# Who multiplies an edge's one-hot by its digits: VectorE as before, or GpSimd

## The reference, cut to what matters

```python
h = _L0_tok_ref(x, ...)                                   # (64, 64, 64): 4096 nodes
h = h + _L0_attn_ref(_layernorm(h), ...)                  # window attention, 8 heads of 8
h = h + _L0_ffn_ref(_layernorm(h), ..., L0_ffn_edge_index)

# inside _L0_ffn_ref: a graph attention over the edges decides each node's experts
src = concatenate([edge_index[0], loops]); dst = concatenate([edge_index[1], loops])
e = leaky_relu(a_src[src] + a_dst[dst], 0.2)
ee = exp(e - segment_max(e, dst)[dst])
alpha = ee / (segment_sum(ee, dst)[dst] + 1e-16)
agg = segment_sum(h[src] * alpha[:, :, None], dst) + b_gat
```

## Time and profile before

| what | value |
|---|---|
| median of the runs | 905.33 us |
| profiled execution, its own time | 901.5 us |
| its span, first to last instruction | 899.7 us |
| busy in the span: TensorE, VectorE, ScalarE, GpSimd | 64%, 65%, 30%, 37% |
| window attention, first key product to last subtraction | 72.0 to 307.2 us |
| of it, chunks made by VectorE | 186.3 to 268.8 us |

### The profile page before, as it was taken

One profiled execution on the slowest core, in us unless ns is written; L12 is line 12 of the kernel. 1 busy time (PEld: TensorE's weight loads), 2 busy tenths in 40 slices (PEclk: granted clock), 3 DMA queues, 4 the chain that ended last, 5 costly groups with the idle time before them and its releaser, 6 DMA issues. The chain is left out here.

```text
span 899.7 us, 12066 instructions
## 1 busy us (share of the span) xinstructions
PE 573.7 (64%) x4179; PEld 341.4 (38%) x4179; DVE 582.3 (65%) x1272; ACT 267.7 (30%) x485; POOL 337.4 (37%) x387
## 2 busy tenths in 40 slices
PE   5427779666789764154665346561875774588886
PEld 4314446344566454022222122210874552422332
DVE  7976999999995675587556264637443336555663
ACT  1133223122224331033323031321015343365553
POOL 5023123122334222667774677750003210224344
PEclk9996555556689755565555655555556995579998
DMA  6100000000000003212121111100000000000001
GB/s 175 27 1 1 1 1 1 1 0 2 1 1 1 3 1 50 39 21 37 23 37 32 9 32 29 23 7 0 1 0 1 1 1 1 0 1 0 13 13 24
DMA packets 29161, 13.74 MB, mean 15 GB/s; under 512 B 22353, under 2 KB 26290, under 8 KB 28851
## 3 DMA queue, kind: packets, MB, share of 16 engines
q1 hardware_dynamic: 23858, 11.35, 5.0%
q0 software_dynamic: 5248, 1.68, 2.6%
HBM read 11.46 MB, written 1.55 MB: 14 GB/s over the span
## 5 line engine op out<-in xcount | busy, mean ns | idle before, releaser
L1423 POOL DMA_INDIRECT edge_src_row<-src_rows_dram,slot_src_index x160 | 173.5, 1084 | 57.4 <-issue 48.0
L600 POOL TENSOR_TENSOR wa_scores<-wa_scores,wa_max 128x512 f32<-128x512 f32 x32 | 37.1, 1160 | 160.9 <-DVE wa_max L781 160.9
L491 POOL TENSOR_TENSOR ln_xs<-xn,ln_stats 128x256 f32<-128x256 f32 x32 | 21.2, 672 | 153.5 <-DVE ln_stats L459 94.3
L645 PE MATMUL wa_s_ps<-wa_kbd,wa_qk 64*64 64x512 f32 x128 | 54.9, 945 | 27.4 <-issue 27.4
L544 PE MATMUL ln_pT<-ident,ln_xs 128*64 128x128 f32 (+1 forms) x112 | 27.7, 410 | 49.2 <-POOL ln_xs L491 48.5
L1537 PE MATMUL moe_h_ps<-xT,moe_w 65*128 65x512 f32 x64 | 57.0, 1041 | 0.0
L2016 POOL TENSOR_TENSOR moe_acc<-moe_acc,moe_weighted 128x512 f32<-128x512 f32 x28 | 37.8, 1349 | 47.4 <-DVE moe_weighted L1957 47.3
L1265 DVE TENSOR_TENSOR edge_e<-edge_src_row,edge_dst_row 128x40 f32<-128x40 f32 x16 | 3.2, 200 | 76.3 <-DMA edge_src_row<-src_rows_dram,slot_src_index 76.2
L1957 DVE SCALAR_TENSOR_TENSOR moe_weighted<-moe_y_ps,moe_b_cols,moe_G 128x512 f32<-128x512 f32 x32 | 24.0, 751 | 42.9 <-ACT moe_G L1930 40.7
L738 ACT ACTIVATE wa_probsT<-wa_t_ps 128x512 f32<-128x512 f32 x32 | 19.1, 597 | 105.9 <-PE wa_t_ps L653 105.9
L113 DVE TENSOR_TENSOR edge_scratch<-edge_scratch,last_dst_lo 128x3072 bf16<-128x3072 bf16 x28 | 49.0, 1751 | 0.0
(11 more groups left out here) (377 smaller groups left out, 1425.1 us busy)
## 6 DMA issues: line engine op xcount, KB each, us to landing
edge_onehot_T<-slot_lo_dram SPq DMA_DIRECT2D x16, 320.0 KB, 3.5
edge_src_row<-src_rows_dram,slot_src_index POOLq DMA_INDIRECT x160, 2.5
edge_scratch<-in_L_ffn_edge_index SPq DMA_DIRECT2D x2, 1024.0 KB, 6.1
xrow<-in_x SPq DMA_DIRECT2D x4, 256.0 KB, 7.9
out_h<-h SPq DMA_DIRECT2D x4, 256.0 KB, 2.6
moe_w<-in_L_ffn_W SPq DMA_DIRECT2D x3, 256.0 KB
src_rows_dram<-src_rows SPq DMA_DIRECT2D x1, 320.0 KB
moe_w<-in_L_ffn_W SPq DMA_DIRECT2D x2, 128.0 KB
```

The lines of the kernel that those rows point to most:

```text
L600: pool.tensor_tensor(sc[b][:], sc[b][:], bc(mx[b][:], WIN), ALU.subtract).then_inc(shifted, 1)
L645: ins = pe.matmul(s_ps[b][half], qk[b][half, 0, :], kbd[b][half])
L1423: pool.indirect_dma_start(gs[b][:, j, :], None, srow_dram, bass.IndirectOffsetOnAxis(edges.src_index[:, x:x + 1], axis=0))\
```

## The change

The two multiplications of a chunk go from VectorE to GpSimd. GpSimd's loop over pairs of tiles is written out, tile by tile, since the work now differs from tile to tile, and a new function `weigh(pool, c)` is called after `shift(c)`; it does something for c = 15 to 24 only, two chunks in each. The unweighted columns get a second buffer, as two engines now share them. A new semaphore `at_ready` tells GpSimd that a chunk's columns are compared, another, `weighed`, counts GpSimd's multiplications; VectorE waits for it before it writes a buffer of columns again, and TensorE before its matmuls. The generator's condition on `now` is restated.

```diff
--- before.py
+++ after.py
@@ -603,13 +603,10 @@
                 keys(b, b, True)
             for b in range(2):
                 shift(b, b)
-            with pool.Fori(0, n // 2 - 2) as i:
-                for b in range(2):
-                    keys(2 * i + b + 2, b, False)
-                    shift(2 * i + b + 2, b)
-            for b in range(2):
-                keys(n - 2 + b, b, False)
-                shift(n - 2 + b, b)
+            for c in range(2, n):
+                keys(c, c % 2, False)
+                shift(c, c % 2)
+                edges.weigh(pool, c)
 
         @block.tensor
         def _(pe):
@@ -851,10 +848,10 @@
         self.lim = mem.sb("edge_limits", [P, 2], I32)
         self.limits = mem.sb("edge_trips", [P, 2], I32)
         (self.loaded, self.step, self.reduced, self.counted, self.found_more, self.passed, self.filled,
-         self.bucketed, self.prefixed, self.move_ready, self.moved, self.decoded, self.turned, self.turned_out,
+         self.bucketed, self.prefixed, self.at_ready, self.weighed, self.move_ready, self.moved, self.decoded, self.turned, self.turned_out,
          self.lo_stored, self.onehot_ready) = (mem.sem("edges_" + x) for x in (
              "loaded", "step", "rest_reduced", "rest_counted", "more_found", "vector_waits_passed", "reach_filled",
-             "bucketed", "prefixed", "move_ready", "moved", "decoded", "lo_turned", "lo_turned_out", "lo_stored",
+             "bucketed", "prefixed", "at_ready", "weighed", "move_ready", "moved", "decoded", "lo_turned", "lo_turned_out", "lo_stored",
              "onehot_ready"))
         self.done = 0
         self.now = -1
@@ -880,8 +877,9 @@
         self.to_col = [room[:, b * col:(b + 1) * col].bitcast(F16)\
                        .rearrange("p (y c q x) -> p y c q x", y=2, c=GCH // 2, x=2) for b in range(RING)]
         room = room[:, RING * col:]
-        self.at_col = room[:, 0:col // 2].bitcast(F16).rearrange("p (c q x) -> p c q x", c=GCH // 2, x=2)
-        room = room[:, col // 2:]
+        self.at_col = [room[:, b * col // 2:(b + 1) * col // 2].bitcast(F16)\
+                       .rearrange("p (c q x) -> p c q x", c=GCH // 2, x=2) for b in range(2)]
+        room = room[:, col:]
         self.move16 = [room[:, x * RC:(x + 1) * RC].bitcast(F16) for x in range(4)]
 
     def constants(self, pool):
@@ -1030,18 +1028,16 @@
         for j in range(FOUND_CHUNKS):
             assert self.now < MOVE_STEP + j // MOVES, (j, self.now)
             wide = PER * (reach(j)[1] - reach(j)[0])
-            while self.now <= MOVE_STEP + (j - RING) // MOVES:
+            while self.now <= MOVE_STEP + (j - RING) // MOVES or self.now < MOVE_STEP - 2 + j // MOVES:
                 take_last()
                 yield
             if j >= RING:
                 dve.wait_ge(self.moved, j - RING + 1)
             part, iota = slice(GCH * j, GCH * j + GCH), self.iota_rep[:]
-            row, col, at = self.to_row[j % RING], self.to_col[j % RING], self.at_col[:, :, 0:wide]
-            equal(dve, row, iota, row16[:, part]).then_inc(self.move_ready, 1)
-            self.after(dve, equal(dve, at, iota, col16[:, part]))
-            weighted_by(dve, col[:, 0, :, 0:wide], at, high16[:, part]).then_inc(self.move_ready, 1)
-            self.after(dve, weighted_by(dve, col[:, 1, :, 0:wide], at, low16[:, part]))
-            dve.sem_inc(self.move_ready, 1)
+            equal(dve, self.to_row[j % RING], iota, row16[:, part]).then_inc(self.move_ready, 1)
+            if j > 1:
+                dve.wait_ge(self.weighed, 2 * j - 2)
+            equal(dve, self.at_col[j % 2][:, :, 0:wide], iota, col16[:, part]).then_inc(self.at_ready, 1)
             yield
 
         while self.now < TURN_STEP:
@@ -1097,6 +1093,19 @@
         self.after(dve, dve.tensor_copy(self.last_lo[:], digit))
         yield
 
+    def weigh(self, pool, c):
+
+
+        if MOVE_STEP <= c < MOVE_STEP + FOUND_CHUNKS // MOVES:
+            for j in range(MOVES * (c - MOVE_STEP), MOVES * (c - MOVE_STEP + 1)):
+                part, wide = slice(GCH * j, GCH * j + GCH), PER * (reach(j)[1] - reach(j)[0])
+                pool.wait_ge(self.at_ready, j + 1)
+                if j >= RING:
+                    pool.wait_ge(self.moved, j - RING + 1)
+                col, at = self.to_col[j % RING], self.at_col[j % 2][:, :, 0:wide]
+                weighted_by(pool, col[:, 0, :, 0:wide], at, self.move16[2][:, part]).then_inc(self.weighed, 1)
+                weighted_by(pool, col[:, 1, :, 0:wide], at, self.move16[3][:, part]).then_inc(self.weighed, 1)
+
     def multiply(self, pe, c, k):
 
 
@@ -1111,7 +1120,8 @@
         if MOVE_STEP <= c < MOVE_STEP + FOUND_CHUNKS // MOVES:
             for j in range(MOVES * (c - MOVE_STEP), MOVES * (c - MOVE_STEP + 1)):
                 low, high = reach(j)
-                pe.wait_ge(self.move_ready, 3 * (j + 1))
+                pe.wait_ge(self.move_ready, j + 1)
+                pe.wait_ge(self.weighed, 2 * j + 2)
                 for i in range(GCH):
                     ins = pe.matmul(slots[:, :, PER * low:PER * high], self.to_row[j % RING][:, i // 2, :, i % 2],
                                     self.to_col[j % RING][:, :, i // 2, 0:PER * (high - low), i % 2], start=False,
```

## The result

| | before | after |
|---|---|---|
| median of 4 runs each | 905.87 us (904.64 to 911.16) | 943.44 us (937.93 to 947.49) |
| ratio of the times | 1 | 1.0399, 95% interval 1.0326 to 1.0472 |
| profiled execution, span | 901.5, 899.7 us | 937.9, 936.1 us |

What follows compares the result with a forecast made beforehand. The prediction took VectorE to bound attention where it has list work, elsewhere a ring of dependent steps. Longer intervals (+34) and clock recovery (+0.5) on 905.3 gave 940 us; range 918 to 955, the forecast's own 931 to 949.

Steps and rivals of the forecast that it cites:

- The weighing: The forty multiplications moved to GpSimd, four per tile for tiles 15 to 24, predicted to delay the next tile's keys.
- the ring: Window attention's dependent steps: GpSimd's subtraction and keys, TensorE's scores, VectorE's bias and maximum; 4.75 us per turn at clock 1.00.
- Its price: GpSimd's time for the forty multiplications, at 1.69 ns an element plus 0.178 us each: 47.1 us back to back.
- Both rivals on the price: GpSimd's multiplication at half price, 0.84 ns an element (919 us, chance 0.10), or dearer, 2.3 ns (955 us, 0.10).
- The turns: GpSimd's operations and VectorE's comparisons exclude each other at SBUF: 1.1 us per weighing interval, 7.7 us over intervals 17 to 24.
- The clock: TensorE's granted clock in the attention stage, said to decide between totals of +28.1 and +35.2 us.
- the slow end: The total taken for a low granted TensorE clock in the long attention intervals: +34 us.
- Interval 19: From GpSimd's subtraction of tile 19 to the next; predicted at some 12.5 to 13.3 us instead of 8.4.
- the ring of 5.64: One turn of the dependent attention steps with 0.70 of TensorE's clock granted, against 4.75 us at 1.00.
- Intervals 14 to 16: Attention stretches between GpSimd's subtractions: 14 loses four multiplications, -1.1 us; 15 and 16 gain +2.8 us behind VectorE's wait.
- The unrolling is free: Writing out GpSimd's attention loop was taken as 0 us, with up to 2 kept for the range.
- Hidden in GpSimd's idle time: Rival: the multiplications fit into GpSimd's 68.5 us of waiting for VectorE's maximum, giving 884 us; chance 0.05.

Runs made afterwards that it cites:

- twice: The changed kernel, but GpSimd does each of its 40 multiplications twice, writing the same values again; ratio 1.0907 to the kernel before.
- half: The changed kernel, but GpSimd multiplies by the high digit only and VectorE by the low one; ratio 1.0105 to the kernel before.
- order_buffers: The changed kernel with four buffers of unweighted columns and GpSimd's multiplications moved after keys(c+1), before shift(c+1); ratio 1.0013 to the kernel before.
- takes_first: The kernel before, with VectorE's MAX8 and MATCH_REPLACE8 moved ahead of the comparisons in tiles 13 to 15; ratio 0.9979 to the kernel before.
- buffers: The changed kernel with four buffers of unweighted columns instead of two, GpSimd's order unchanged; ratio 1.0386 to the kernel before.
- unroll: The kernel before with GpSimd's window attention loop written out tile by tile, VectorE still multiplying; ratio 0.9997 to the kernel before.

## Why the prediction was right

- **The weighing is in the ring.** Shown by twice and half (0.93 and 0.83 us for one), and from the other side by order_buffers, which takes it out of the ring and gets nearly all of it back.
- **Its price.** 47.1 us were predicted; undisturbed multiplications took 1.58 us for 840 elements and 1.65 for 880 (1.60 and 1.67 by the line through the float32 rows), and 0.58 for 240. With the turns counted in, the group has 50.5. Both rivals on the price, 0.84 and 2.3 ns an element, fall: it is 1.66 to 1.69. One premise of this went unsaid. In all the float32 rows with two inputs, one input is repeated along the tile, as a digit is in `weighted_by`. Where both inputs are full tensors, 512 elements take GpSimd more than 1.04 us, in the same trace of before:

```profile
L2016 POOL TENSOR_TENSOR moe_acc<-moe_acc,moe_weighted x28: 1260/1270/1652, 805.8 to 892.4; 128x512 f32<-128x512 f32 x28
```

By that row, 2.1 ns an element with the same fixed part, the weighing would have come out some 11 us dearer (an estimate). The rows chosen were the ones alike, but the prediction gives no reason for choosing them; whether the repeated input makes the difference was not tested.
- **The turns.** 0.37 and 0.45 us at the fourth multiplication and the keys, where I had 0.35 and 0.43. takes_first shows that they come from VectorE's comparisons. The way to the 0.43 was wrong, and its size partly luck: the 1.42 us show 0.14 us hidden, not 0.26, as 0.52 us of the comparison were left when the subtraction started and it grew by 0.38. The keys met not 0.69 us of a comparison but 0.59: the comparison had itself waited and ended at 249.90, the fourth multiplication at 249.34.
- **The clock.** I took the slow end. Interval 19 came to 13.16 (I had said 12.5 to 13.3), 17 to 24 to 92.9 (86.1 to 93.2), with 0.67 granted. The scores of interval 19 took 1.97 us instead of 1.08, and these 0.89 us are all that parts the ring of 5.64 from that of 4.75. After them interval 25 took 5.64 instead of 4.75, 0.9 where I had put 0.5; but not for the reason given. The clock was at 0.95 and the scores took 1.08 us. It is the keys that started late, as the queries that they need came late from TensorE through ScalarE:

```profile
311.67 1.04 POOL L594 TENSOR_TENSOR wa_kbd<-wa_qk,headmask 128x512 f32<-128x512 f32 x1 [0.84 <-ACT wa_qk L712]
```

- **Intervals 14 to 16.** 7.75, 10.42 and 12.15; I had 8.15, 10.7 and 12.5. That VectorE's wait costs at 15 and 16, as the sum has it, is what buffers shows.
- **The unrolling is free.** Shown.
- **The forecast's distance.** The total was +34.5 against +37.6 by medians and +36.4 by profiles. The stage accounts for 33.9 in intervals 14 to 24 and 0.9 in the rest; the 1.6 us left lie outside these intervals and were not looked into.
- **Hidden in GpSimd's idle time** (the rival on the faster side) is wrong for this program. Its mechanism is real with another order and more buffers, but its price was not: even then GpSimd's own work is as long as what VectorE was relieved from, and the turns come on top (order_buffers, interval 19).

## What to carry to other kernels

Idle time of an engine that waits for the answer to its own work is not room. Before moving work into it, follow its program order and ask whether what others wait for is queued behind the new work. Two edits that each remove one of two waits in parallel may have to be made together to show anything. Where VectorE and GpSimd take turns at SBUF, moving an operation from the one to the other makes the exclusive time longer (here 1.65 against some 0.6 us for 880 elements); it is better to put VectorE's operations with one SBUF input beside GpSimd's work.

## What the runs showed of the hardware that was not expected

At a granted clock of 0.50 TensorE itself became the bound of an attention interval without other work. The interval then took 6.36 us, all of it busy, where 4.75 are needed at 1.00. The low clock can stay for several intervals (in half this one and the next, 6.36 and 6.78 us). A window of half:

```profile
308.30:314.66 6.36, 6.36 (x43) 3.90 (x41) 2.03 (x5) 1.84 (x7) 2.04 (x2) 0.50 0.01 3
```

The ring at the slow clock is still 5.64 us; what comes on top in this window is that the scores start 0.8 us after the keys have ended, behind TensorE's other work. In the long intervals with weighing TensorE has time left (busy for 6.87 of 13.16 us at 19), and there 5.64 was the right figure.

And the same program took 2 to 3% more in the three later comparisons than in the first one, with a spread of 16 to 23 us within one, though the stage of unroll took the same time as that of before to 0.4 us. The record doesn't show whether the chip is the cause. A difference of less than 1% had to be read from the intervals first.
